# Attention and expert layer on one core: bias additions, scatters, fetches and two folds moved, last block by heads

## The reference, cut to what matters

```python
xn = _layernorm(x, axis=-1)
# attention, 16 heads of 64 over all 2048 tokens, no mask
q, k, v = xn @ Wq, xn @ Wk, xn @ Wv            # by heads
attn = softmax(einsum('bqhd,bkhd->bhqk', q, k) * SCALE)
a = einsum('bhqk,bkhd->bqhd', attn, v).reshape(b, s, H * DH) @ Wo + bo
# experts: each token goes to the one expert with the highest logit
h = square(relu(einsum('btd,edh->ebth', xn, expert_fc)))
out_e = einsum('ebth,edh->ebtd', h, expert_proj)      # masked to the chosen expert
return x + a + f
```

## Time and profile before

| | us |
|---|---|
| median of 3 executions | 1330.27 (1330.06 to 1330.44) |
| profiled execution: its own time | 1330.05 |
| profiled execution: its span | 1328.3 |
| TensorE busy | 1316.0 (99%) |
| VectorE busy | 1212.3 (91%) |
| GpSimd busy | 1132.8 (85%) |
| ScalarE busy | 695.6 (52%) |

### The profile page before, as it was taken

One profiled execution on the slowest core, in us unless ns is written; L12 is line 12 of the kernel. 1 busy time (PEld: TensorE's weight loads), 2 busy tenths in 40 slices (PEclk: granted clock), 3 DMA queues, 4 the chain that ended last, 5 costly groups with the idle time before them and its releaser, 6 DMA issues.

```text
span 1328.3 us, 20241 instructions
## 1 busy us (share of the span) xinstructions
PE 1316.0 (99%) x6192; PEld 857.2 (65%) x6192; DVE 1212.3 (91%) x1907; ACT 695.6 (52%) x1210; POOL 1132.8 (85%) x902
## 2 busy tenths in 40 slices
PE   8999999999999999999999999999999999999998
PEld 6765556766667666677666676666766667765554
DVE  8989999999999899998999989999899989999897
ACT  5654446644456544466444565444654445654453
POOL 7899999877898778997788977888878879789998
PEclk9999999999999999999999999999999999999999
DMA  5242323342333423234122432224322234021101
GB/s 140 59 114 60 86 60 92 70 99 53 82 77 71 107 50 82 66 93 101 42 74 66 109 86 50 76 65 102 91 54 73 67 86 108 19 66 45 35 18 40
DMA packets 148700, 97.46 MB, mean 73 GB/s; under 512 B 83760, under 2 KB 114160, under 8 KB 148592
## 3 DMA queue, kind: packets, MB, share of 16 engines
q1 hardware_dynamic: 147568, 94.06, 29.0%
q0 software_dynamic: 1024, 2.10, 0.5%
HBM read 34.34 MB, written 13.63 MB: 36 GB/s over the span
## 4 chain that ended last, share of the span: by engine, by line
PE 88%; POOL 7%; DVE 3%; issue 2%; DMA 0%; ACT 0%; POOLq 0%; DVEq 0%
PE OB L1304 30%; PE SB L1244 16%; PE SB L1253 16%; PE MB L1272 16%; POOL acc L604 5%; PE XB L1346 2%; PE XB L1232 2%; PE XB L1225 2%; PE XB L1311 1%; PE XB L1312 1%; PE XB L1313 1%; DVE mx L892 1%; POOL sorted_x L661 1%; POOL K L667 0%; PE OB L1207 0%
## 5 line engine op out<-in xcount | busy, mean ns | idle before, releaser
L604 POOL TENSOR_TENSOR acc<-acc,ex 128x512 f32<-128x512 f32 x691 | 913.0, 1350 | 31.1 <-ACT ex L760 0.7
L892 DVE TENSOR_REDUCE mx<-MB 128x1 f32<-128x512 f32 x992 | 639.9, 679 | 36.8 <-PE MB L1272 36.5
L760 ACT ACTIVATE ex<-SB 128x512 f32<-128x512 f32 x1024 | 607.3, 599 | 119.9 <-PE SB L1253 55.6
L1304 PE MATMUL OB<-ex,V 128*64 128x512 f32 x2048 | 447.2, 594 | 0.0
L1244 PE MATMUL SB<-Q,K 128*128 128x512 f32 x1024 | 407.9, 399 | 0.2 <-ACT ex L760 0.2
L1253 PE MATMUL SB<-Q,K 128*128 128x512 f32 x1024 | 399.3, 390 | 0.0
L1272 PE MATMUL MB<-K,Q 128*128 128x512 f32 x992 | 390.5, 394 | 3.8 <-DVE mx L892 3.8
L1304 PEld LDWEIGHTS OB<-ex,V 128*64 128x64 f32 x2048 | 144.1, 137 | 277.6 <-issue 274.0
L928 DVE TENSOR_TENSOR acc<-acc,ex 128x512 f32<-128x512 f32 x205 | 304.0, 1483 | 21.0 <-POOL acc L604 2.3
L790 ACT ACTIVATE osb<-OB 128x512 f32<-128x512 f32 x32 | 19.1, 598 | 449.1 <-PE OB L1304 449.1
L1244 PEld LDWEIGHTS SB<-Q,K 128*128 128x128 f32 x1024 | 192.5, 188 | 67.3 <-issue 27.6
(11 more groups left out here) (171 smaller groups left out, 650.6 us busy)
## 6 DMA issues: line engine op xcount, KB each, us to landing
Q<-high SPq DMA_DIRECT2D x124, 128.0 KB, 2.3
K<-high SPq DMA_DIRECT2D x112, 128.0 KB, 2.3
Q<-low SPq DMA_DIRECT2D x62, 128.0 KB, 2.3
rd<-rows_rd SPq DMA_DIRECT2D x62, 128.0 KB, 2.9
K<-low SPq DMA_DIRECT2D x56, 128.0 KB, 2.3
v_rows<-xT SPq DMA_DIRECT2D x112, 64.0 KB, 1.9
w<-fc SPq DMA_DIRECT2D x23, 256.0 KB, 2.7
w<-projT SPq DMA_DIRECT2D x23, 256.0 KB, 3.1
```

Source lines behind the costliest of these rows:

```text
L604: pool.tensor_tensor(a[:, :], src[:, :], EX[h][kt][:, :], ALU.add).then_inc(done, 1)
L760: act.activation(EX[h][kt][:, :], SB[bank_of(n, 2 * kt + h)][:, :], ACT.Exp).then_inc(a_e[h], 1)
L892: dve.tensor_reduce(mx[:, m % 2, u:u + 1], MB[bank_of(m, i)][:, :], AX.X, ALU.max).then_inc(v_m, 1)
L1304: mm = pe.matmul(OB[own[h], :], V[:, k, own[h]], EX[h][k][:, :], start=(k == 0), stop=(k == NT - 1))
```

## The change

- The bias additions leave the ends of blocks 0 to 3 and go to blocks 4 to 7, behind key tile 2. They now come after `sum_up` of the same quarter, four blocks earlier.
- Block 0: VectorE adds tile 10 of head 0 as well, GpSimd one tile less.
- Scatters: five, four and seven in blocks 1, 2 and 3, where there were six, four and six. Fetches: five, six and five in blocks 28, 29 and 30, where there were five, seven and four.
- Blocks 2 and 3 leave `LATE`: head 1 is folded right behind head 0, ahead of the next block's maxima.
- The last block's denominators and projections are made and used head by head.

```diff
-SORT = [(1, kt) for kt in (2, 4, 6, 8, 10, 12)] + [(2, kt) for kt in (2, 4, 13, 14)] + [(3, kt) for kt in (2, 4, 6, 8, 10, 12)]
-FETCH = [(NB - 4, kt) for kt in (4, 6, 8, 10, 12)] + [(NB - 3, kt) for kt in (2, 4, 6, 8, 10, 12, 14)] + [(NB - 2, kt) for kt in (2, 4, 6, 8)]
-LATE = (0, 1, 2, 3, NB - 4, NB - 3)
+SORT = [(1, kt) for kt in (2, 4, 6, 8, 10)] + [(2, kt) for kt in (2, 4, 6, 14)] + [(3, kt) for kt in (2, 4, 6, 8, 10, 12, 14)]
+FETCH = [(NB - 4, kt) for kt in (4, 6, 8, 10, 12)] + [(NB - 3, kt) for kt in (2, 4, 6, 8, 10, 12)] + [(NB - 2, kt) for kt in (2, 4, 6, 8, 10)]
+LATE = (0, 1, NB - 4, NB - 3)
...
-            first = 11 if n.off == 0 else 9 if n.off in (1, 2, 3, NB - 4, NB - 3, NB - 2) else 10
+            first = 10 if n.off == 0 else 9 if n.off in (1, 2, 3, NB - 4, NB - 3, NB - 2) else 10
...
                 def add_bias(j):
-                    pool.wait_ge(*normalised(j))
+                    pool.wait_ge(v_y, j + 1)
...
-                    if n.off < JB:
-                        add_bias(n.off)
+                        if JB <= n.off < 2 * JB and kt == 2:
+                            add_bias(n.off - JB)
...
                     if n.off < JB:
-                        dve.wait_ge(g_y, n.off + 1)
+                        dve.wait_ge(*normalised(n.off))
+                    elif n.off < 2 * JB:
+                        dve.wait_ge(g_y, n.off - JB + 1)
...
+                    for h in range(2):
+                        heads = slice(h * TB, (h + 1) * TB)
+                        dve.wait_ge(t_den, h + 1)
+                        dve.reciprocal(rd[:, heads], LAST_DEN[h][:, 0:TB]).then_inc(v_rd, 1)
+                        dve.wait_ge(v_rd, h + 1)
+                        dve.wait_ge(v_back, 1)
+                        dve.wait_ge(t_wo, NB + h)
+                        for q in range(TB):
...
                     for h in range(2):
                         wait(pe, sums[h][n % 2], added(n, NT - 1))
-
-                    for q in range(TB):
-                        for h in range(2):
-                            mm = pe.matmul(XB[:, 2 * q + h:2 * q + h + 1], acc[h][n % 2][:, q * P:(q + 1) * P], ones[:, 0:1],
+                        if h == 0:
+                            pe.wait_ge(v_m, UNITS * NB)
+                        for q in range(TB):
+                            mm = pe.matmul(LAST_DEN[h][:, q:q + 1], acc[h][n % 2][:, q * P:(q + 1) * P], ones[:, 0:1],
                                            start=True, stop=True)
-                    mm.then_inc(t_den, 1)
-                    pe.wait_ge(a_o, NB)
...
+                        mm.then_inc(t_den, 1)
+                        if h == 0:
+                            pe.wait_ge(a_o, NB)
+                        for q in range(TB):
+                            mm = pe.matmul(LAST_WO[h][:, q * P:(q + 1) * P], osb[own[h], q * P:(q + 1) * P],
                                            wo_s[(PAIRS - 1) % 2][own[h], :], start=True, stop=True)
-                        if q % 2:
-                            mm.then_inc(t_wo, 1)
+                        mm.then_inc(t_wo, 1)
```

More of the change, by code:

```diff
@@ L315, in layer @@
         FIRST_S = 3
-        LAST = [SB[0:2], MB[0:2]]
+        LAST_DEN, LAST_WO = [XB, MB[2]], MB[0:2]
         def k_ready(eng, pair):
@@ L1157, in last @@
                 def last():
[L1159 to L1176 removed]
+                    for h in range(2):
[6 more added lines that the diff above has]
+                        for q in range(TB):
+                            y = Y[:, NT - TB + q, :]
+                            if h:
+                                dve.wait_ge(v_y0, q + 1)
+                            dve.scalar_tensor_tensor(out=y, in0=LAST_WO[h][:, q * P:(q + 1) * P], scalar=rd[:, h * TB + q:h * TB + q + 1],
+                                                     in1=y, op0=ALU.mult, op1=ALU.add).then_inc((v_y0, v_y)[h], 1)
                 schedule(dve, first, one, last)
@@ L1442, in last @@
                         wait(pe, sums[h][n % 2], added(n, NT - 1))
-                    for q in range(TB):
-                        for h in range(2):
-                            mm = pe.matmul(XB[:, 2 * q + h:2 * q + h + 1], acc[h][n % 2][:, q * P:(q + 1) * P], ones[:, 0:1],
+                        if h == 0:
+                            pe.wait_ge(v_m, UNITS * NB)
+                        for q in range(TB):
+                            mm = pe.matmul(LAST_DEN[h][:, q:q + 1], acc[h][n % 2][:, q * P:(q + 1) * P], ones[:, 0:1],
                                            start=True, stop=True)
-                    mm.then_inc(t_den, 1)
-                    pe.wait_ge(a_o, NB)
-                    pe.wait_ge(v_m, UNITS * NB)
-                    for q in range(TB):
-                        for h in range(2):
-                            mm = pe.matmul(LAST[q // 2][h][:, q * P:(q + 1) * P], osb[own[h], q * P:(q + 1) * P],
+                        mm.then_inc(t_den, 1)
[3 more added lines that the diff above has]
+                            mm = pe.matmul(LAST_WO[h][:, q * P:(q + 1) * P], osb[own[h], q * P:(q + 1) * P],
                                            wo_s[(PAIRS - 1) % 2][own[h], :], start=True, stop=True)
-                        if q % 2:
-                            mm.then_inc(t_wo, 1)
+                        mm.then_inc(t_wo, 1)
                 schedule(pe, first, one, last)
```

16 lines of the change are left out of this document (removed).

## The result

| | before | after |
|---|---|---|
| median, 19 executions each | 1330.27 (1330.06 to 1331.21) | 1332.53 (1330.91 to 1334.85) |
| ratio, 95% interval | | 1.0017 (1.001 to 1.0024) |
| profiled execution, own time | 1330.05 | 1331.36 |
| its span | 1328.32 | 1329.63 |
| TensorE / VectorE / GpSimd busy | 1316.0 / 1212.3 / 1132.8 | 1317.3 / 1215.2 / 1132.3 |

The account below looks back on a forecast made before the run. The prediction took TensorE, with 88% of the chain of waits, to bound the kernel. Its terms summed to +0.2 us on 1330.05, giving 1330.25; with 0.22 for the median it forecast 1330.5 us, no change, range 1328.0 to 1332.6.

Parts of the forecast that it names:

- Blocks 1 and 2: Blocks 1 and 2: GpSimd gets early enough that VectorE's late folds no longer wait for it; minus 0.93 and minus 0.61 us.
- the term -1.1: Block 3: with head 1 folded ahead of the maxima, it loses 0 to 0.2 us instead of 1.20.
- the prediction's own rule: Blocks 3 and 4: what TensorE gains in block 3 it waits for in block 4; together they lose 2.0 us.
- GpSimd's end is fixed from E2: Block 3: GpSimd, gated by ScalarE, ends 42.8 us after block 2's end; block 4's maxima wait, plus 3.05 us there.
- Blocks 4 to 7: Blocks 4 to 7: the moved bias falls into GpSimd's idle time at a block's start; cost 0, at most 0.3 us.
- TensorE's half of the end gets 1.0 us plus some 0.1 from the work by heads: The end: block 30's vanished wait gives TensorE 1.0 us, the last block's work by heads some 0.1.
- GpSimd's half: The end: GpSimd gains only what it waited for ScalarE in block 31; the end as a whole minus 0.2 us.
- The sum: Whole kernel: -0.93 - 0.61 - 1.1 + 3.05 + 0 - 0.2 = +0.2 us, no change; chance 0.68.
- The clock: the rival: Block 4: TensorE's wait of some 3.5 us brings its clock down, costing 1 to 2 us, 1331.5 to 1332.5; chance 0.14.

Follow-up runs that it names:

- old end: Changed kernel with the last block's denominators, projections and VectorE additions as in the kernel before; 1332.10 us, ratio 1.0012.
- late fold: Changed kernel with block 3 alone put back in `LATE`; 1329.84 us, ratio 0.9993.
- the changed kernel again: Changed kernel with no edit, run once more beside others on one chip; 1333.16 us, ratio 1.0011.
- dense fill: Changed kernel with twelve unused matmuls of 512 columns ahead of unit 3 of block 4, in TensorE's wait; 1330.99 us, ratio 1.0002.
- thin fill: Changed kernel with ten unused matmuls of 128 columns ahead of unit 3 of block 4, in TensorE's wait; 1331.90 us, ratio 1.0007.
- heads in turn: Changed kernel with the last block's projections of both heads in turn, tile by tile, denominators still by head; 1331.62 us, ratio 1.0004.
- the fetches alone: Kernel before with only the fetches as in the changed kernel (five, six, five); 1330.30 us, ratio 0.9994.
- six scatters: Changed kernel with the scatters of the kernel before (six, four, six); 1331.02 us, ratio 1.0001.
- the best sum: Kernel before with bias in blocks 8 to 11, block 0's addition on VectorE, block 2 out of `LATE`, fetches five, six, five; 1328.22 us, ratio 0.9979.
- folds only: Kernel before with only blocks 2 and 3 taken out of `LATE`; 1332.68 us, ratio 1.0011.
- the kernel before by heads: Kernel before with only the last block's denominators and projections made head by head; 1331.66 us, ratio 1.0005.
- bias only: Kernel before with only the bias moved to blocks 4 to 7 and block 0's one addition given to VectorE; 1330.55 us, ratio 0.9997.

## Why the prediction came out as it did

**Blocks 1 and 2: right.** Forecast -0.93 and -0.61, measured -0.94 and -0.63. The bias and block 0's addition do it without the rest of the change; the two were not run apart.

**Block 3: the term -1.1 was mis-sized, it measured -0.26 in after.** GpSimd ended block 2 at E2 + 0.71 instead of E2 - 0.5 to E2 - 0.2, so that VectorE's fold waited for it until E2 + 0.75. It had waited 0.69 us for the reciprocals (up to 0.3 was allowed), and its ten additions ahead of the last scatter took 15.23 us, where they took 14.80 with the late fold. Seven profiles are of kernels that are the same program up to the end of block 3. By GpSimd's wait for the reciprocals they stand in order: none with the old end, where block 3 took 38.86 us, 0.28 (late fold) with 39.09, 0.35 (the changed kernel again) with 39.18, 0.51 (dense fill) with 39.32, 0.69 (after) with 39.78 and 0.76 (thin fill) with 39.79; with the heads in turn, where the rows show no such wait, it took 38.94. So the gain is 0.25 to 1.18 us from execution to execution, and the forecast was its upper end. It hardly matters to the sum, by the prediction's own rule: what block 3 gains block 4 loses. The three of these kernels whose fold stood early and whose clock stayed up have 81.51, 81.48 and 81.39 us for both blocks.

**Blocks 3 and 4 together: right.** The step "GpSimd's end is fixed from E2" forecast +2.0 (1.7 to 2.4) from E2 on, and +2.16 was measured. GpSimd ended at E2 + 43.1 against E2 + 42.8. The scatter measured 1.1 us (E2 + 43.1 against E2 + 42.0 with six), as taken. Putting block 3 back into `LATE` took 2.6 us off the two blocks. TensorE stood 2.77 us where 3.5 was forecast, as block 3 was longer; with a block 3 of 38.9 it stood 3.5.

**Blocks 4 to 7: right for this kernel.** Blocks 5 to 7 took 41.39, 41.37 and 39.98 us, before 41.42, 41.40 and 39.97. That it is the long block 4 that hides the first bias, as the prediction said, fits the other kernels. Where block 4 is short the bias costs something in the block behind it: 0.34 us alone, 0.78 with block 3 back in `LATE`, 0.69 with the bias in block 8, against the 0.3 allowed.

**The end: the step "TensorE's half of the end gets 1.0 us plus some 0.1 from the work by heads" failed.** TensorE's half did get the 1.0 from block 30 (0.98). The work by heads does not give 0.1, it takes 0.8 to 0.9 us (shown alone in the kernel before). On TensorE the reason is shown: the eight projections of one head take 1.16 us where both heads in turn took that together, so the last one ends 4.1 us after the block instead of 2.9. I had counted matmuls and not which rows of the array they use. But that is not all of it. With TensorE's order mended and VectorE still working by heads the tiles left no earlier (4.71 against 4.69); with the old order on both they left 3.91 after the block. How the 0.8 splits between the two engines stays open. In after's profile the clock fell in those very projections and they took another 0.67 (1.83 less 1.16). Net the end measured +0.54 (block 30, block 31 and the rest) where -0.2 was forecast. GpSimd's half was mis-sized too. Counted from the start of block 30, which came 0.77 us later than before, GpSimd's three additions began 1.17 earlier, took 0.45 longer and ended 0.72 earlier, where 0.2 was forecast; the fetches alone gave the same 0.7. The prediction had counted too little of what GpSimd lost in block 31 of the kernel before: 0.70 us of waiting for ScalarE and 0.39 on its first addition.

**The sum.** Terms of blocks 1 to 4 +0.59 (forecast +0.41), the end +0.54 (forecast -0.2), the start +0.19 (not forecast, and within what profiles without a fall there differ by, 76.24 to 76.55): the +1.3 of the profiled execution.

**The clock: the rival came true in part of the executions, and its chance of 0.14 was too low.** The other 0.95 us of the median go with executions that have a lower mean clock: six of after's 19 took 1330.9 to 1331.6 us at 0.997 or 0.998, thirteen 1332.2 to 1334.9 at 0.997 down to 0.995. That a fall in block 4 does this is shown by the profiles with the old end (+2.1 us for 6.83 us at half clock), of the changed kernel again (+1.0 for 3.41) and by the filled wait, which took 1.5 us off the mean. The price of 1 to 2 us was as forecast. It was taken from the earlier trace rows, whose 24 small matmuls the prediction read as the lower level. The profile's clock column says 1.00 there, so that reading rested on their lengths alone; the changed kernel again bears it out, where eight matmuls of that shape took 1.91 us at 0.50 from 39.85 on, and in after 1.05 at 1.00. I had treated the fall as an alternative to the worked-out sum; it comes on top of it, in some executions and not in others. How large its share is in the 19 executions is argued from the clusters, not shown, since only one of them was profiled; falls ahead of block 0 (below) take part in them too, but those the kernel before most likely has as well. That the rule of the Trainium skill which the prediction quoted (TensorE: Matmul & The Clock Gate, "Why this matters for your kernels") applies is what the traces bear out, but not as a limit of length: the clock stayed up after 2.77 us of standing (after) and fell after 2.63 (six scatters), 3.29 (the changed kernel again), 3.50 (heads in turn) and 3.53 (old end). The fall came between 0.8 us before TensorE resumed (old end) and 0.8 after (the changed kernel again). None of the runs shows what decides.

## What to carry to other kernels

Work moved ahead of a queue must be done by the time the queue starts: find the time at which its producer can end at the earliest, and if a gate fixes that, gains upstream only lengthen the wait. A wait of the bounding engine has two prices, itself and the clock that it may bring down afterwards; the second shows only in part of the executions, so profile more than one and read the clusters of times beside the median. Before work is split by heads or halves, see which of its pieces ran side by side: matmuls that use half of the array's rows each gain only in turn with those of the other half. And see whether the engine behind them takes their results in an order that lets it start.

## What the runs showed of the hardware that was not expected

- **The clock also falls ahead of block 0,** near 36 us, with TensorE busy with sparse small matmuls (groups of four of 8 columns in 0.51 us). The same rows stand in profiles without a fall. Five of the fourteen have it, for 3.41 us (late fold, thin fill, the best sum) or 6.83 us (folds only, the changed kernel again), and block 0 then ends at 77.8 or 79.5 to 79.6 instead of 76.2 to 76.6. Up to there the kernel with the folds alone is the kernel before. The 33 executions of before in the first group lie 20 near 1330.3, 9 near 1331.1 and 4 near 1332.7 us. The two steps, 0.8 and 2.4, are less than the 1.5 and 3.3 us by which block 0 ends later; the profile with the folds alone gives 0.5 of that back in block 1. That the clusters are these falls is thus likely, and not shown: before's own profile had none.
- **It falls at the end** in all fourteen profiles, in after at 1324.13, with TensorE at work 1.00 of the time in the windows shown. It cost 0.67 us there, and as much with the dense fill, where the last projections took 1.83 us as well. In before it fell at 1324.74, after TensorE's last matmul (1324.02), where it costs nothing.
- **GpSimd's additions take longer beside VectorE's.** GpSimd's three last additions took 3.71 us in before and 3.70 in the kernel before by heads, where VectorE's last addition had ended (at 1319.43, ahead of 1320.52, in before). They took 4.16 wherever they began while it still ran, and it is the first of the three that takes it, 1.71 us in after against 1.26 in before: in after (1320.12, VectorE's from 1319.13 for 1.58), with the old end, and with the fetches alone (1319.37, VectorE's from 1318.38 for 1.57). An engine that comes earlier may meet the other's work.
- **One row stays unexplained.** VectorE's `up<-tile_no,end` took 1.00 us in after and 1.39 with the folds only, but 0.34 in before, with the bias only, with the heads only and with the fetches only. The four short ones are the kernels in which block 2 is in `LATE`; why that should matter no run shows. GpSimd was adding beside it in before as well (196.55 for 4.18).
